# A new order of all engines, two products in four column tiles, and the expert turns written out

## Chip, core and metric

The kernel runs on one core of a Trainium2 chip (trn2). The metric is the device time of one execution in microseconds, median of three runs of the kernel before: 1279.1 us (1278.93 to 1279.16). Less is better.

## What is computed

128 samples; each has 64 image patches, one class token and 32 text tokens of width 128, so 97 tokens.

```python
h = concat(tokens(x), txt)                     # patches @ W, + b, * positions; 97 tokens of 128
h = h + retention(layernorm(h))                # complex, 8 heads of 16, decay mask, group norm, gate
h = h + ffn(layernorm(h))
def ffn(x):
    o = softmax(q k^T / 4) v @ Wo + bo         # 8 heads of 16
    t = layernorm(x + o)
    e, gw = argmax, max of softmax(t @ gate_W + gate_b)
    return gw * (gelu(t @ W1[e] + b1[e]) @ W2[e] + b2[e])      # one of 8 experts per token
```

All of it is float32.

## The kernel before

Four samples make a group (388 tokens); there are NG = 32 groups. The first stage is a software pipeline over groups, written out by hand for each engine: one iteration `i` of `for i in range(FIRST, STEADY)` is a list of steps, each for the group `i - lag` (`at(step, i - lag)`). After the loop each engine has a list of its own for the last groups. Nothing but the order in these lists and the semaphores sets the order of the work. The steps with A are the first attention, B the second, C the third normalization and the routing.

- TensorE: `ahead(g, c0, c1)` is part of the embedding of a coming group (19 chunks of 128x128 weights by 256 columns, L479). `a_scores`, `b_scores`, `b_shifted` (L550, L614, L637) use four row tiles of 32 rows of the array. `a_mix`, `b_mix`, `b_sums` (L564, L667, L649) use four column tiles of 32 columns. All else uses the whole array, among it `product` (L460) with 128x128 weights by 388 columns: `a_q_real`, `a_q_imag`, `a_gate`, `a_out`, `b_q`, `b_k`, `b_wo`. `b_hrows` is L681, `c_rows` L690, `b_max_t` L624, the bfloat16 `c_rank` L698 and L701. A float32 product is two matmul instructions in the trace, a float32r one is one.
- PSUM has eight banks: emb, x, y, z and s0 to s3. `USES` and `LAST_USES` name the bank of each step. A step waits until the holder before it has been drained.
- VectorE: `a_decayed` and `b_max` over 776 columns, the routing (`place_all` to `place_index`, which gives the row in HBM of each token), and more.
- ScalarE: logs, exponentials, and the copies out of PSUM into `row_sb`: `b_row_copy` (L1120) and `c_row_copy` (L1127). `row_sb` has ROWS = 3 buffers, so both wait in `free_rows(g)` until the scatter of group g - 3 has landed.
- GpSimd: `text(g)` copies text tokens; `scatter(g)` (L1909) writes the rows of group g to HBM (`expert_rows`), four indirect DMAs of 97 rows. It waits for `place_index(g)`, the gate weight, the token numbers and `b_row_copy(g)`.

In the second stage 104 tiles of 128 tokens, 13 turns of 8 slots, go through the expert network: TensorE turns a tile (L825), makes the hidden layer (L832) and the output (L843); VectorE copies weights (L1844, L1846) and makes the result (L1853 to L1859); GpSimd writes it to the output with an indirect DMA (L1926). In `result(n, s)` of a turn n > 0 VectorE waits until the output of the same slot in the turn before has landed. TensorE's turns 0, 1 and 12, and VectorE's too, are written out; the others are loops of the hardware (`Fori`), ScalarE's from turn 1 on. The expert phase begins when `place_index(NG - 1)` and `run_on(NG - 1)` are done.

The lines that set the two waits which matter below:

```python
def free_rows(g):
    if g >= ROWS:
        act.wait_ge(s_scat[g % ROWS], 16 * G * (g // ROWS))
...
def result(n, s):
    ...
    if later(n):
        dve.wait_ge(s_out[s], 16 * n)
```

Of the kernel before, what the change touches and what calls it, by code (L numbers as in the profile page):

```python
# [55 lines left out]
def _pack(*fields):  # L56
# [35 lines left out]
    ("A.scores2.0", "s0 s1", NG - 1), ("A.scores2.1", "s2 s3", NG - 1), ("B.q", "y", NG - 2), ("B.o", "z", NG - 3),  # L92
    ("A.scores3.0", "s0 s1", NG - 1), ("A.scores3.1", "s2 s3", NG - 1), ("B.den", "y", NG - 3),
    ("B.scores1.0", "s0 s1", NG - 2), ("B.scores1.1", "s2 s3", NG - 2), ("B.scores0.0", "s0 s1", NG - 2),
    ("B.scores0.1", "s2 s3", NG - 2), ("A.yvar", "y", NG - 1), ("B.wo", "z", NG - 3), ("B.v", "s0", NG - 2),
    ("B.max_t0", "y", NG - 2), ("B.hrows", "x", NG - 2), ("A.out", "s2", NG - 1), ("C.rank", "z", NG - 4),
    ("B.max_t1", "s3", NG - 2), ("C.rows0", "s0", NG - 3), ("C.rows1", "s1", NG - 3), ("B.center", "y", NG - 1),
    ("B.shifted1.0", "s0 s1", NG - 2), ("B.shifted1.1", "s2 s3", NG - 2), ("B.var", "z", NG - 1),
    ("B.shifted0.0", "s0 s1", NG - 2), ("B.shifted0.1", "s2 s3", NG - 2), ("B.k", "z", NG - 1), ("B.q", "s2", NG - 1),
    ("B.den", "s1", NG - 2), ("C.rank", "s0", NG - 3), ("B.o", "y", NG - 2), ("B.scores1.0", "s0 s1", NG - 1),  # L100
    ("B.scores1.1", "s2 s3", NG - 1), ("B.wo", "y", NG - 2), ("B.max_t1", "z", NG - 1),
    ("B.scores0.0", "s0 s1", NG - 1), ("B.scores0.1", "s2 s3", NG - 1), ("C.rows1", "y", NG - 2),
    ("C.rows0", "x", NG - 2), ("B.max_t0", "z", NG - 1), ("B.shifted1.0", "s0 s1", NG - 1),
    ("B.shifted1.1", "s2 s3", NG - 1), ("B.shifted0.0", "s0 s1", NG - 1), ("B.shifted0.1", "s2 s3", NG - 1),
    ("B.v", "x", NG - 1), ("B.den", "s1", NG - 1), ("B.o", "x", NG - 1), ("C.rank", "s2", NG - 2),
    ("B.wo", "z", NG - 1), ("C.rows0", "s0", NG - 1), ("C.rows1", "s3", NG - 1), ("B.hrows", "z", NG - 1),
    ("C.rank", "s0", NG - 1),
]
STEADY = NG
# [24 lines left out]
def counts(order):  # L134

    seen, n = {}, 0
    for i in range(FIRST, LAST):
        for *what, lag in order:
            if 0 <= i - lag < NG:
                n += 1  # L140
                seen[(i - lag, *what)] = n
    return seen
# [3 lines left out]
    ("exp_sum", 4), ("place_all", 4), ("place_chosen", 4), ("place_sum", 4), ("place_index", 4), ("logit_max", 3),  # L146
    ("top", 3), ("top_index", 3), ("first_top", 3)]
ROUTE = counts(ROUTE_ORDER)
# [13 lines left out]
def fusion(nc, x_main, x_tail, w_main, w_tail, txt_t, pos_t, consts, weights, columns, token_no,  # L162
           exp_w1, exp_w2, no_token, out, rows, table):
    with ExitStack() as ctx:
# [286 lines left out]
        def _(pe):  # L451
# [75 lines left out]
            def a_q_real(g):  # L527
                read(pe, g, "A.center")
                product(g, "A.qr", ar[:], xn[:, g % 2, :])

            def a_q_imag(g):
                read(pe, g, "A.center")
                product(g, "A.qi", ai[:], xn[:, g % 2, :])

            def a_gate(g):
                read(pe, g, "A.center")
                product(g, "A.gate", weight("w1"), xn[:, g % 2, :])
# [37 lines left out]
            def a_out(g):  # L575
                pe.wait_ge(s_yn, g + 1)
                product(g, "A.out", weight("w2"), yn[:])
# [7 lines left out]
            def b_q(g):  # L585
                read(pe, g, "B.center")
                product(g, "B.q", weight("Wq"), x2[:, g % 2, :])

            def b_k(g):
                read(pe, g, "B.center")  # L590
                product(g, "B.k", weight("Wk"), x2[:, g % 2, :])

            def b_values(g):
                read(pe, g, "B.center")
                ps = use(g, "B.v")
                for c in range(4):
                    mm = pe.matmul(ps[0:S, c * P:(c + 1) * P], x2[:, g % 2, c * S:(c + 1) * S], weight("Wv"),  # L597
# [277 lines left out]
        def _(act):  # L875
# [368 lines left out]
            for s in range(SLOTS):  # L1244
                hidden(0, s)
# [791 lines left out]
```

## Time and profile before

| | |
|---|---|
| median of 3 runs | 1279.1 us |
| the profiled execution | 1277.0 us, its span 1275.0 us |
| TensorE busy | 97% (matmuls), weight loads 73% |
| VectorE, ScalarE, GpSimd busy | 78%, 62%, 32% |
| DMA | 98 GB/s in the mean, 16 engines a third busy |
| mean granted TensorE clock | 0.991 |

The span is the time from the first instruction to the last in the profiled execution; 2 us lie around it. Busy shares are of the span. The granted clock is a share of full speed: 1.00 is 2.4 GHz, 0.50 is 1.2 GHz. The chain of work is followed back from the last instruction, at each step to what released it.

### The profile page before, as it was taken

The numbers are of one execution on the slowest core, as the hardware profiler recorded it, in microseconds if no ns is written. First come the engines' busy times: TensorE is split into PE (matmuls) and PEld (weight loads), VectorE is DVE, ScalarE is ACT, GpSimd is POOL, SyncE is SP. The second block draws the span as 40 slices with busy tenths as digits, with TensorE's granted clock in tenths as the row PEclk, the third lists the DMA queues.
The fourth block names the chain that finished last, engine by engine and source line by source line (L and its number), as shares of the span: only waits on it lengthen the run. The fifth ranks groups of instructions, "written<-read, shape, count | busy, mean of one in ns | idle before, by whom it ended". The sixth has DMA issues, their size and how long they took to land.

```text
span 1275.0 us, 43269 instructions
## 1 busy us (share of the span) xinstructions
PE 1240.5 (97%) x15924; PEld 930.4 (73%) x15925; DVE 998.1 (78%) x2447; ACT 794.3 (62%) x1787; POOL 410.5 (32%) x268
## 2 busy tenths in 40 slices
PE   8999999999999999999999999999999876999998
PEld 6667777777777777777777777777776556999998
DVE  3678888888888888888888888888888766777776
ACT  2466666666666666666666666666666664556555
POOL 0000322232222222222222222222222146666666
PEclk9999999999999999999999999999999898999999
DMA  9522333333333333333333333333330013443332
GB/s 387 188 83 80 93 93 93 93 93 93 93 93 93 93 93 93 93 93 93 94 92 93 93 93 94 93 93 94 93 93 16 14 17 89 135 114 102 103 103 62
DMA packets 95146, 124.80 MB, mean 98 GB/s; under 512 B 56619, under 2 KB 77149, under 8 KB 94592
## 3 DMA queue, kind: packets, MB, share of 16 engines
q1 hardware_dynamic: 38400, 102.47, 25.4%
q0 software_dynamic: 56576, 19.93, 7.5%
q8 instruction: 122, 2.00, 0.7%
q14 instruction: 48, 0.39, 0.1%
HBM read 101.27 MB, written 20.82 MB: 96 GB/s over the span
## 4 chain that ended last, share of the span: by engine, by line
PE 80%; DVE 6%; issue 5%; DVEq 3%; POOL 2%; DMA 2%; ACT 1%; SPq 0%; POOLq 0%; ACTq 0%
PE bank_emb L479 22%; PE bank_s L550 10%; PE bank_x L564 7%; PE bank_y L460 7%; PE bank_s L637 4%; PE bank_s L614 4%; PE bank_z L460 4%; PE bank_y L649 3%; PE bank_y L667 3%; DVEq L1842 2%; PE bank_z L597 2%; DVE home_x L1846 2%; PE bank_s L460 2%; PE bank_y L690 1%; PE bank_s L843 1%
## 5 line engine op out<-in xcount | busy, mean ns | idle before, releaser
L1909 POOL DMA_INDIRECT expert_rows<-row_sb,placei x128 | 278.1, 2173 | 562.8 <-issue 464.8
L479 PE MATMUL bank_emb<-home_x 128*128 128x256 f32 x1216 | 338.1, 392 | 0.0
L479 PEld LDWEIGHTS bank_emb<-home_x 128*128 128x128 f32 x1216 | 210.3, 189 | 81.9 <-issue 56.5
L1374 DVE TENSOR_TENSOR home_s<-bank_s,con 97x776 f32<-97x776 f32 x256 | 239.3, 956 | 22.9 <-PE bank_s L550 22.8
L1926 POOL DMA_INDIRECT out_tokens<-yo,tok x104 | 122.9, 1181 | 69.7 <-issue 52.7
L1391 DVE TENSOR_REDUCE mx<-bank_s 97x8 f32<-97x776 f32 x128 | 117.7, 961 | 30.8 <-PE bank_s L614 30.6
L1102 ACT ACTIVATE home_s<-bank_s 97x776 f32<-97x776 f32 x128 | 97.5, 814 | 59.5 <-PE bank_s L637 59.5
L550 PE MATMUL bank_s<-qm,xn 32*97 32x452 f32 x1024 | 131.4, 580 | 1.7 <-DVE vp L1381 1.2
L564 PEld LDWEIGHTS bank_x<-home_s,vp 97*32 97x32 f32 x4096 | 90.0, 110 | 33.2 <-issue 29.4
L564 PE MATMUL bank_x<-home_s,vp 97*32 97x97 f32 x4096 | 111.8, 249 | 1.2 <-DVE vp L1381 1.2
L843 PE MATMUL bank_s<-w2e,home_s 128*128 x832 | 109.8, 275 | 0.0
L843 PEld LDWEIGHTS bank_s<-w2e,home_s 128*128 128x128 f32 x832 | 101.3, 192 | 0.0
L1241 ACT ACTIVATE home_s<-bank_x,home_x 128x128 f32<-128x128 f32 x208 | 59.3, 367 | 46.6 <-PE bank_x L832 37.5
L1241 ACT ACTIVATE home_s<-bank_y,home_x 128x128 f32<-128x128 f32 x208 | 59.3, 368 | 43.8 <-PE bank_y L832 39.3
L1381 DVE COPY vp<-bank_s 97x128 f32<-97x128 f32 x256 | 67.5, 284 | 23.5 <-PE bank_s L550 23.1
L1896 POOL COPY h<-txt 128x128 f32<-128x128 f32 x32 | 9.4, 292 | 230.2 <-DVE h L1429 206.6
L550 PEld LDWEIGHTS bank_s<-qm,xn 32*97 32x97 f32 x1024 | 34.2, 158 | 45.0 <-issue 36.5
L637 PE MATMUL bank_s<-qx,kx 32*97 32x97 f32 x2048 | 60.9, 255 | 3.5 <-ACT home_s L1102 1.7
L637 PEld LDWEIGHTS bank_s<-qx,kx 32*97 32x97 f32 x2048 | 50.4, 162 | 19.0 <-issue 14.6
L614 PE MATMUL bank_s<-k,q 32*97 32x194 f32 x1024 | 60.3, 341 | 1.2 <-DVE mx L1391 0.7
L1066 ACT ACTIVATE kx<-bank_z,kx_bias,con 128x194 f32<-128x194 f32 x128 | 59.5, 528 | 2.5 <-PE bank_z L460 2.5
L832 PE MATMUL bank_x<-home_s,home_x 128*128 128x128 f32 x416 | 56.5, 280 | 3.2 <-DVE home_x L1846 3.0
(297 smaller groups left out, 2369.9 us busy)
## 6 DMA issues: line engine op xcount, KB each, us to landing
home_x<-in_x_main SPq DMA_DIRECT2D x96, 768.0 KB, 4.5
home_x<-expert_rows SPq DMA_DIRECT2D x104, 129.0 KB
w1e<-in_exp_w SPq DMA_DIRECT2D x1, 2576.0 KB, 13.2
txt<-in_txt_t SPq DMA_DIRECT2D x32, 64.0 KB, 3.6
w2e<-in_exp_w SPq DMA_DIRECT2D x1, 2048.0 KB, 17.6
expert_rows<-row_sb,placei POOLq DMA_INDIRECT x128, 8.7
out_tokens<-yo,tok POOLq DMA_INDIRECT x104
home_x<-in_x_tail SPq DMA_DIRECT2D x32, 48.0 KB, 3.4
```

Of the source, the lines that this page charges most:

```text
L460: done(pe.matmul(ps[:, 0:N], lhs, rhs, start=True, stop=True), g, name)
L479: mm = pe.matmul(banks["emb"][:, 0:NPG], wtok[:, c, :], x_sb[:, c, :], start=(c == 0), stop=(c == KC - 1))
L550: mm = pe.matmul(bank_s[0:S, r, 0:4 * S + 64], xn[rows32, g % 2, t], qm[rows32, k, :], start=True, stop=True)
L564: mm = pe.matmul(ps[32 * r:32 * r + 32, k * S:(k + 1) * S], v, sm[:, k % 2, r, j * S:(j + 1) * S], start=(j == 0), stop=(j == 3), skip_gro ...
L614: mm = pe.matmul(dst, q2[rows32, t], k2[rows32, :, t], start=True, stop=True)
L637: mm = pe.matmul(bank_s[0:S, r, j * S:(j + 1) * S], kx[rows32, o, t], qx[rows32, o, t], start=True, stop=True)
L843: mm = pe.matmul(banks[bank_o[s % 2]][:, 0:P], hid[:, s, f, :], w[:, f * P:(f + 1) * P], start=(f == 0), stop=(f == FB - 1))
L1241: act.activation(hid[:, s, f, :], banks[bank_h[s % 2]][:, f * P:(f + 1) * P], ACT.Gelu_apprx_tanh, bias=w1b[:, s, FF + f:FF + f + 1]).then ...
L1374: ins = dve.tensor_tensor(sm[:, k % 2, 2 * h:2 * h + 2, :], pair(h), decay, ALU.mult)
L1391: drain(dve.tensor_reduce(mx[:, k, :].rearrange("p (r j z) -> p r j z", j=4, z=8)[:, 2 * h:2 * h + 2, :, 0], pair(h).rearrange("p g (j t) ...
L1909: pool.indirect_dma_start(out=rows[:, :], out_offset=bass.IndirectOffsetOnAxis(ap=placei[:, k, c:c + 1], axis=0), in_=row_sb[:, k, c, E:E ...
L1926: pool.indirect_dma_start(out=out, out_offset=bass.IndirectOffsetOnAxis(ap=tok[:, s, :], axis=0), in_=yo[:, s, :], in_offset=None, bounds_ ...
```

## The change

1. All lists of steps, for TensorE, ScalarE, VectorE and GpSimd, have another order, and so have `USES`, `LAST_USES` and the numbering of routing steps. The loop ends an iteration sooner (`STEADY = NG - 1`), the lists for the end are longer by it. ScalarE and VectorE start their iteration at another point of the cycle.
2. `b_q` and `b_k` are made in four column tiles (`split=True`), beside `b_sums`, `b_mix` and `a_mix`.
3. `place_index(g)` comes later on VectorE, behind `b_normal` and `c_scale`; `place_all` and `place_chosen` come sooner. Two waits are added (`logits` for the exponentials of the group before, `place_sum` for the `place_index` of the group before).
4. GpSimd's scatters at the end come in another order.
5. The expert turns of TensorE, VectorE and ScalarE are written out instead of looped.

```diff
-            def product(g, name, lhs, rhs):
+            def product(g, name, lhs, rhs, split):
                 ps = use(g, name)
-                done(pe.matmul(ps[:, 0:N], lhs, rhs, start=True, stop=True), g, name)
+                for c in range(0, P, 32) if split else ():
+                    mm = pe.matmul(ps[c:c + 32, 0:N], lhs[:, c:c + 32], rhs, start=True, stop=True)
+                if not split:
+                    mm = pe.matmul(ps[:, 0:N], lhs, rhs, start=True, stop=True)
+                done(mm, g, name)
```

TensorE's loop afterwards (the loop before is printed above):

```python
a_scores(i-1, 2); ahead(0, 1); b_sums(i-3, 0), (1); a_mix(i-1, 1); a_scores(i-1, 3)
b_q(i-2, split=True); b_mix(i-3, 0); a_mix(i-1, 2); b_mix(i-3, 1); a_mix(i-1, 3)
b_scores(i-2, 1); a_center(i); ahead(1, 3); b_wo(i-3); ahead(3, 5); a_var(i); c_rank(i-4); ahead(5, 7)
b_scores(i-2, 0); a_yvar(i-1); ahead(7, 8); a_q_real(i); c_rows(i-3, 0); ahead(8, 9); b_max_t(i-2, 1)
b_hrows(i-2); c_rows(i-3, 1); a_q_imag(i); b_shifted(i-2, 1); a_out(i-1); ahead(9, 10); b_values(i-2)
a_scores(i, 1); ahead(10, 12); b_center(i-1); b_max_t(i-2, 0); ahead(12, 13); a_gate(i)
a_scores(i, 0); ahead(13, 15); b_var(i-1); ahead(15, 18); b_shifted(i-2, 0); ahead(18, 19)
a_mix(i, 0); b_k(i-1, split=True)
```

```diff
-    ("B.scores1.1", "s2 s3", 2), ("B.wo", "y", 3), ("A.var", "s2", 0),
-    ("B.max_t1", "s0", 2), ("B.hrows", "y", 2), ("C.rows1", "x", 3), ("B.shifted1.0", "s0 s1", 2),
+    ("C.rows0", "z", 3), ("B.max_t1", "s1", 2), ("B.hrows", "s0", 2), ("C.rows1", "z", 3), ("A.qi", "x", 0),
+    ("B.shifted1.0", "s0 s1", 2), ("B.shifted1.1", "s2 s3", 2), ("A.out", "z", 1), ("B.v", "y", 2),
...
 # ScalarE, loop
-                at(a_query, i, 1)
-                at(a_query, i, 0, last=True)
-                at(b_row_copy, i - 2)
-                at(c_row_copy, i - 3, 1)
-                at(b_exp, i - 2, 1, 0)
+                at(y_rstd, i)
+                at(a_query, i + 1, 0)
+                at(c_row_copy, i - 2, 0)
+                at(a_query, i + 1, 1, last=True)
+                at(b_row_copy, i - 1)
+                at(c_row_copy, i - 2, 1)
+                at(c_square, i - 2)
...
 # VectorE, loop
-                at(place_all, i - 4)
-                at(run_on, i - 4)
-                at(place_chosen, i - 4)
-                at(place_sum, i - 4)
-                at(h0_low_ahead, i)
-                at(gate_weight, i - 4)
-                at(place_index, i - 4)
-                at(a_decayed, i - 1, 3, 0)
...
                 at(b_normal, i - 1)
-                at(gate_times, i)
-                at(tokens_ahead, i + 1)
                 at(c_scale, i - 3)
+                at(place_index, i - 4)
                 at(logits, i - 3)
...
 # GpSimd
             for i in range(FIRST, STEADY):
+                at(text, i + 1)
                 at(scatter, i - 4)
-                at(text, i + 1)
-
+
+            scatter(NG - 5)
             scatter(NG - 4)
+            scatter(NG - 1)
+            scatter(NG - 2)
             scatter(NG - 3)
-            scatter(NG - 2)
-            scatter(NG - 1)
...
 # TensorE, expert turns (VectorE and ScalarE alike)
-            with pe.Fori(2, TURNS1) as n:
+            for n in range(2, TURNS1):
                 turn(n)
             pe.wait_ge(s_list, 2)
-            with pe.Fori(TURNS1, TURNS - 1) as n:
-                turn(n)
-            turn(TURNS - 1, True)
+            for n in range(TURNS1, TURNS):
+                turn(n, n == TURNS - 1)
```

## Rows read from the trace of the kernel before

**Rows 1.** The page, section 1: busy time, share of the span, instructions.
```profile
PE 1240.5 (97%) x15924; PEld 930.4 (73%) x15925; DVE 998.1 (78%) x2447; ACT 794.3 (62%) x1787; POOL 410.5 (32%) x268
```

**Rows 2.** Chain of work, one steady iteration: start us, us, what.
```profile
433.35 1.06 PE bank_emb L479 x4
...
434.59 0.18 PE bank_z L468
434.76 1.73 PE bank_emb L479 x8
...
440.40 1.46 PE bank_y L649 x32
...
456.61 0.46 PE bank_x L690 x4
457.07 0.87 PE bank_s L637 x32
...
465.02 1.06 PE bank_emb L479 x4
```

**Rows 3.** Timeline of a steady iteration, VectorE, ScalarE, GpSimd: start us, us, engine.
```profile
444.20 0.14 DVE L1546 CAST placei<-placef 97x4 int32<-97x4 f32 x1
...
467.64 0.56 DVE L1334 TENSOR_TENSOR x<-bank_x,rsb 128x388 f32<-128x388 f32 x1 [0.28 <-ACT rsb L923]
...
456.70 0.59 ACT L1120 COPY row_sb<-bank_y 97x512 f32<-97x512 f32 x1
...
445.58 2.17 POOL L1909 DMA_INDIRECT expert_rows<-row_sb,placei  x1 [17.30 <-issue]
...
452.97 2.15 POOL L1909 DMA_INDIRECT expert_rows<-row_sb,placei  x1 [0.30 <-issue]
```

**Rows 4.** L1909: landing after the start, all; then two windows, a group's fourth.
```profile
DMA to landing us min/median/max: 6.9/8.7/12.5
...
DMA to landing us min/median/max: 12.5/12.5/12.5
...
DMA to landing us min/median/max: 10.2/10.2/10.2
```

**Rows 5.** Timeline around the first expert turns: last placement, scatters, first outputs.
```profile
1061.73 0.17 DVE L1546 CAST placei<-placef 97x4 int32<-97x4 f32 x1
...
1061.46 2.15 POOL L1909 DMA_INDIRECT expert_rows<-row_sb,placei  x1 [6.37 <-DVE place L1519]
...
1081.14 1.00 POOL L1926 DMA_INDIRECT out_tokens<-yo,tok  x1 [0.30 <-issue]
...
1090.02 0.15 DVE L1857 COPY tok<-home_x 128x1 int32<-128x1 int32 x1 [2.23 <-DMA out_tokens<-yo,tok]
...
1091.54 1.16 PE L832 MATMUL bank_x<-home_s,home_x 128*128 128x128 f32 x8 [1.27 <-DVE home_x L1846]
```

**Rows 6.** Windows: stretch, its length, busy time of PE, PEld, DVE, ACT, POOL, clock, DMA.
```profile
950.00:1061.50 111.50, 94.29 (x1451) 63.10 (x1450) 83.74 (x221) 69.20 (x141) 35.22 (x18) 0.95 0.12 22
...
1005.00:1010.00 5.00, 5.00 (x59) 2.27 (x62) 1.52 (x8) 4.37 (x8) 0.00 (x0) 0.54 0.00 0
...
1101.30:1118.00 16.70, 16.30 (x139) 15.59 (x137) 11.63 (x41) 9.28 (x33) 9.48 (x8) 1.00 0.47 129
...
1133.10:1148.40 15.30, 15.30 (x139) 15.30 (x137) 11.19 (x40) 9.13 (x33) 9.68 (x9) 1.00 0.36 103
```

**Rows 7.** TensorE's timeline: the fill, the last iteration of the loop, two expert tiles.
```profile
41.57 1.02 PE L550 MATMUL bank_s<-qm,xn 32*97 32x452 f32 x8 [0.94 <-DVE vp L1381]
...
977.71 1.02 PE L550 MATMUL bank_s<-qm,xn 32*97 32x452 f32 x8
...
1007.87 1.84 PE L550 MATMUL bank_s<-qm,xn 32*97 32x452 f32 x8
...
1095.44 1.06 PE L832 MATMUL bank_x<-home_s,home_x 128*128 128x128 f32 x8
...
1097.33 1.06 PE L832 MATMUL bank_y<-home_s,home_x 128*128 128x128 f32 x8
```

More of the change, by code:

```diff
@@ L131, with counts @@
     take(_g, _use)
-def counts(order):
+def counts(order, last):
     seen, n = {}, 0
-    for i in range(FIRST, LAST):
+    for i in range(FIRST, STEADY):
         for *what, lag in order:
@@ L573, in a_yvar, with a_out @@
                 halves(g, "A.yvar", "sqy", mean_head_r[:], y_hi[:], y_lo[:])
-            def a_out(g):
+            def a_out(g, split=False):
                 pe.wait_ge(s_yn, g + 1)
-                product(g, "A.out", weight("w2"), yn[:])
+                product(g, "A.out", weight("w2"), yn[:], split)
             def b_center(g):
@@ L596, in b_values @@
                 for c in range(4):
-                    mm = pe.matmul(ps[0:S, c * P:(c + 1) * P], x2[:, g % 2, c * S:(c + 1) * S], weight("Wv"),
-                                   start=True, stop=True)
+                    for a in range(0, S, 32 if split else S):
+                        b = min(a + 32, S) if split else S
+                        mm = pe.matmul(ps[a:b, c * P:(c + 1) * P], x2[:, g % 2, c * S + a:c * S + b], weight("Wv"),
+                                       start=True, stop=True)
                 done(mm, g, "B.v")
@@ L682, in b_hrows, with c_rows @@
                 done(mm, g, "B.hrows")
-            def c_rows(g, half):
+            def c_rows(g, half, split=False):
                 read(pe, g, "B.wo")
@@ L722, in _ @@
                 at(a_mix, i - 1, 1)
-                at(c_rank, i - 4)
-                at(ahead, i + 1, 0, 1)
-                at(b_q, i - 2)
                 at(a_scores, i - 1, 3)
-                at(ahead, i + 1, 1, 2)
-                at(a_center_ahead, i)
+                at(b_q, i - 2, split=True)
+                at(b_mix, i - 3, 0)
                 at(a_mix, i - 1, 2)
-                at(b_mix, i - 3, 0)
                 at(b_mix, i - 3, 1)
@@ new lines, in _ @@
+            a_mix(NG - 2, 1)
+            b_sums(NG - 4, 0)
+            b_sums(NG - 4, 1)
+            a_scores(NG - 2, 3)
+            b_q(NG - 3, split=True)
+            b_mix(NG - 4, 0)
+            a_mix(NG - 2, 2)
+            b_mix(NG - 4, 1)
+            a_mix(NG - 2, 3)
+            b_scores(NG - 3, 1, first=True)
+            a_center(NG - 1)
+            b_wo(NG - 4)
+            a_var(NG - 1)
+            c_rank(NG - 5)
+            a_yvar(NG - 2)
+            b_max_t(NG - 3, 1)
+            c_rows(NG - 4, 0)
@@ new lines, in _ @@
+            a_q_real(NG - 1)
+            b_scores(NG - 3, 0)
+            b_hrows(NG - 3)
+            c_rows(NG - 4, 1)
+            a_out(NG - 2)
+            a_q_imag(NG - 1)
+            b_shifted(NG - 3, 1)
+            b_max_t(NG - 3, 0)
+            b_values(NG - 3)
+            a_scores(NG - 1, 1, first=True)
+            b_center(NG - 2)
+            a_gate(NG - 1)
+            a_scores(NG - 1, 0)
+            b_var(NG - 2)
+            b_shifted(NG - 3, 0)
+            a_mix(NG - 1, 0)
@@ L768, in _ @@
+            b_k(NG - 2, split=True)
+            a_scores(NG - 1, 2)
             a_mix(NG - 1, 1)
-            b_q(NG - 2)
-            b_mix(NG - 3, 0)
+            b_q(NG - 2, split=True)
             a_scores(NG - 1, 3)
             a_mix(NG - 1, 2)
+            c_rank(NG - 4)
             b_sums(NG - 3, 0)
@@ L1242, in hidden @@
                                    bias=w1b[:, s, FF + f:FF + f + 1]).then_inc(s_gelu, 1)
[L1244 to L1246 removed]
+            for n in range(TURNS):
                 for s in range(SLOTS):
@@ new lines, in _ @@
+            b_query_max(NG - 3, 1, 0)
+            b_query_max(NG - 3, 1, 1, last=True)
+            y_normal(NG - 2)
+            place_sum(NG - 5)
+            y_gated(NG - 2)
+            place_index(NG - 5)
+            b_max(NG - 3, 0, 1)
+            b_max(NG - 3, 0, 0)
+            a_residual(NG - 2)
+            a_query_imag(NG - 1, 0)
+            a_query_imag(NG - 1, 1, last=True)
+            c_sum(NG - 4)
+            h1_low(NG - 2)
+            b_query_max(NG - 3, 0, 1)
+            a_value_rows(NG - 1, 1, 1)
@@ new lines, in _ @@
+            a_decayed(NG - 1, 1, 0)
+            a_value_rows(NG - 1, 1, 0, last=True)
+            a_decayed(NG - 1, 1, 1, last=True)
+            b_query_max(NG - 3, 0, 0, last=True)
+            b_low(NG - 2)
+            gate_one(NG - 1)
+            a_value_rows(NG - 1, 0, 1)
+            a_decayed(NG - 1, 0, 1, last=True)
+            a_value_rows(NG - 1, 0, 0)
+            a_decayed(NG - 1, 0, 0, last=True)
+            b_normal(NG - 2)
+            c_scale(NG - 4)
+            logits(NG - 4)
@@ L1734, in _ @@
             one_hot(NG - 4)
             a_decayed(NG - 1, 3, 1)
-            a_value_rows(NG - 1, 3, 1, last=True)
             a_decayed(NG - 1, 3, 0)
             a_value_rows(NG - 1, 3, 0, last=True)
+            a_value_rows(NG - 1, 3, 1, last=True)
+            place_all(NG - 4)
+            gate_weight(NG - 4)
+            place_chosen(NG - 4)
+            run_on(NG - 4)
+            place_sum(NG - 4)
+            token_numbers(NG - 4)
+            place_index(NG - 4)
+            next(first, None)
```

428 lines of the change are left out of this document (242 added, 186 removed), and 13 rows, old and new, of the table USES.

## Prediction

> **What bounds the kernel.** Read the busy times first: TensorE is busy 97% of the span, VectorE 78%, ScalarE 62%, GpSimd 32% [rows 1]. Then the chain of work over one iteration of the pipeline: it runs through TensorE alone, and an iteration takes 465.02 - 433.35 = 31.67 us [rows 2]. So in the steady stretch, about 30 iterations, only TensorE's own time counts, as long as no other engine makes it wait. Then the timeline of the other engines, for the chains that run beside it [rows 3, 4], and last the expert phase, where tiles follow at 1097.33 - 1095.44 = 1.89 us [rows 7] and where the first turns show a wait on GpSimd [rows 5].
>
> **Part 1: mode switches and the split products.** Eight embedding instructions of 256 columns with no change of tiles ahead of them take 1.73 us, so four need 0.86 and a column 0.84 ns; four behind a row-tiled step take 1.06 [rows 2]. `b_sums`, 32 instructions of 194 columns in four tiles side by side, needs 32 / 4 x 194 x 0.84 ns = 1.31 and takes 1.46 behind row tiles [rows 2]. So each change between whole array, row tiles and column tiles costs about 0.2 us. The old cycle has 19 such changes, the new one 18: `c_rank` no longer stands between column tiles and the whole array, and the split `b_q` joins `b_mix`, but `ahead(0, 1)` now cuts between `a_scores` and `b_sums`. I take -0.14 us an iteration, between 0 and -0.3.
>
> The split itself I cost at nothing: 8 instructions of 388 columns, 0.33 us each by the same rate, need 8 / 4 x 0.33 = 0.65 us in four tiles, what two whole ones need. `b_sums` would need 32 x 0.16 = 5.2 us without overlap and takes 1.46 [rows 2]; so column tiles do run side by side, even with both halves of a product issued one after the other. If they did not here, each product would cost 1 us more, 2 with no overlap at all (a rival).
>
> **Part 2: the wait that the order of VectorE adds.** Here is the step that decides. `row_sb` has three buffers. `b_row_copy(g)` must wait until the scatter of g - 3 has landed, and what waits for the copy is new: `B.hrows` now lies in bank s0, which `b_shifted(g, 1)` takes next, so TensorE itself waits. Behind the waiting copy on ScalarE are queued `c_row_copy`, `c_square` and the exponentials; behind `b_shifted` all of TensorE. Before, `place_index` ran at 444.20 and the fourth DMA of its scatter, started at 452.97, landed near 464; the copy that needed it came at 456.70 + 31.67 = 488.4 [rows 2, 3], 24 us later. Now it stands behind `b_normal` and `c_scale`, a whole iteration later in effect.
>
> The chain, from the end of `b_var` on TensorE (434.59 + 0.18 = 434.77, one iteration on 466.44 [rows 2]): `b_normal` starts 1.20 later at 467.64 [rows 3]; `b_normal` 0.48 and `c_scale` 0.65, an estimate from their rows of that length; `place_index` 0.14; then 444.34 to 445.58 = 1.24 until GpSimd's first DMA starts [rows 3]; 452.97 - 445.58 = 7.39 to the start of the fourth [rows 3]; its landing, 10.2 to 12.5 after its start, 11.35 in the mean of the ten that are recorded, whose ends are shown [rows 4]; the copy, 0.59 [rows 3]; 0.15 for two semaphores. Sum 23.2, from 22.0 to 24.3.
>
> TensorE's own way between the same two steps: before, 457.07 - 434.77 = 22.30 [rows 2]. The same 13 embedding chunks lie in it; one `c_rows` comes in (+0.46 [rows 2]), the saving of part 1 goes out. 22.6. So it waits 0.6 us, and up to 1.7 where a landing is late. The wait returns every time, since `place_index` moves with it. The iteration becomes 31.67 - 0.14 + 0.6 = 32.13, +0.46. It needs g of 3 and more: 26 iterations, +12.0; four others -0.14 each. **Steady: +11.5.** An error of 0.5 us in either sum moves this from about 3 to 24.
>
> Against this stands a rule: the Trainium skill, "DMA: Bandwidth & Descriptors", section "Anatomy of one DMA — SWDGE (gpsimd) path", fits a GpSimd DMA as 2.0 us plus its bytes over 436 KB per us. By that the fourth would land some 2.2 us after its start, the chain would take 14, and nothing would wait. The recorded landings, 8.7 in the median over all [rows 4], do not bear it out for these scattered rows. It belongs to the first rival.
>
> **Part 3: fill and drain.** In the fill TensorE already waits for VectorE between scores and sums, 0.94 us in one place [rows 7]. The new order has one embedding chunk there where the old had more, and less of the second attention to cover it in its first two iterations: +2, from 0 to +4. The iteration without embedding (1007.87 - 977.71 = 30.2 us [rows 7]) loses nine chunks, 3.8 us, from TensorE's way in part 2 but nothing from the chain: it would wait 4.3, of which the old one already loses a part to VectorE: +3, from 0 to +5. The last lists hold the same work with the same last chain; 0, from -4 to +4. The two added waits in the routing hit steps whose releaser ran long before: nothing.
>
> **Part 4: GpSimd's order at the end.** Before, the scatters of groups 30 and 31 start at 1061.46 and the first output DMA at 1081.14, so eight DMAs take 19.68, 2.46 each [rows 5]. It lands 8.9 us on; VectorE waits 2.23 us for it in the first result of turn 1, and TensorE idles 1.27 [rows 5]. Now `scatter(NG - 1)` stands first. It needs the very last `place_index`, whose counterpart is at 1061.73 [rows 5], so 12 DMAs start at 1063.14 and end at 1092.66. **+11.5** for the first output, and VectorE's wait and TensorE's next tile move by the same 11.5. TensorE then idles some 14 us. After gaps of the drain the granted clock was 0.54, near the level of 1.2 GHz, over 5 us [rows 6]; 3 to 7 us at half speed cost 1.5 to 3.5: +2.5.
>
> **Part 5: turns written out.** Turn 2, the first of the loop, took 16.7 us, a later one 15.3 [rows 6]; eight tiles at 1.89 are 15.16. Gain 1.4 + 10 x 0.2 = -3.4. The new code must be fetched; turns 0 and 1 are written out already and show 1.89 [rows 7], so nothing; at worst 0.45 a turn as at a loop's entry, +5. Expert phase: 11.5 + 2.5 - 3.4 = **+10.6**.
>
> **Sum.** 11.5 + 2 + 3 + 0 + 10.6 = +27.1. The profiled execution took 1277.0 and becomes 1304.1; the median lies 2.1 above it: **1306** (1279.1 + 27.1 = 1306.2).
>
> **Rivals.**
> (a) The scatter lands in time; only part 4 costs. For it: the two sums of part 2 are 0.6 apart, each good to 0.5. Then -0.14 x 30 = -4.2, +2, +1, +10.6: +9.4, 1288.5. Chance 0.2.
> (b) Faster: the drain is packed. From 950 to 1061.5 TensorE idles 111.5 - 94.3 = 17.2 us [rows 6]. If the longer lists for the end fill all of it, the last placement comes 17 us sooner, and that outweighs part 4; with no wait of part 2, it decides from 10.6 + 2.6 = 13.2 us on. 17 us give -17 + 10.6 = -6.4: 1272.7. Against it: the last idle stretch is the routing of the last group, one chain in both orders, and VectorE is busy 84 us of that stretch itself. Chance 0.1.
> (c) The split overlaps only in part: each second half waits for its first, five steps of 0.32, so a product takes 1.6 instead of 0.65. The wait of part 2 hides 0.6 of the two; (2 x 0.97 - 0.6) x 30 = +40 on top: 1346. Against it: `b_sums` [rows 2]. The Trainium skill, "TensorEngine Tiling (Array Packing)", section "Restrictions and Gotchas", says that column tiling disables fast weight load; no row here shows that it costs anything. Chance 0.05.
> (d) The pieces cancel, within 0.2% of 1279.1: half of that idle time is filled and (a) holds. Chance 0.05.
>
> **Chances and range.** My forecast 0.60, its own range 1292 to 1324, from the bounds of part 2 (-8.5 to +12.5), of the drain and of the clock. With (a) the range reaches down to 1284 and up to 1324. 0.2% (2.6 us) is about what a measurement of this kernel can tell from no change: faster by more 0.10 from (b), within 0.05 from (d), slower by more 0.85 from the rest.
>
> **What the new profile would show.** Part 1: the cycle without waits at 31.5. Part 2: a wait of TensorE before L637's counterpart each iteration, released by ScalarE's `b_row_copy`, itself released by the scatter; an iteration of 32.1. Part 4: twelve scatters in a row, first output 31 us after the last placement, one idle stretch of about 14 us on TensorE. Part 5: tiles 1.89 apart with no step at turns. Wrong would be: 31.5 with no wait (part 2 is then mis-sized), or more than 33 (landings later than recorded).

## The result and the profile after

| | before | after |
|---|---|---|
| median of the runs, us | 1279.01 (1276.95 to 1279.16) | 1313.76 (1308.95 to 1319.96) |
| profiled execution, us | 1277.0 | 1308.95 |
| its span, us | 1275.0 | 1307.1 |

The changed kernel is slower: ratio 1.028, 95% interval 1.023 to 1.033. The forecast was 1306 with a range from 1284 to 1324. Its runs lie 11 us apart, those of the kernel before, beside them, 2. The profiled execution is the fastest of the four, so what follows explains 32 us of the 34.8 between the medians; what the others lost beyond it is in no profile.

The page of the changed kernel, section 1 (busy time, share, instructions) and parts of section 4 (shares of the chain that ended last). It answers to [rows 1].

```profile
PE 1245.3 (95%) x16308; PEld 926.6 (71%) x16308; DVE 1007.4 (77%) x2446; ACT 791.8 (61%) x1787; POOL 409.8 (31%) x268
...
PE 68%; DMA 11%; POOL 7%; issue 5%; DVE 5%; ACT 3%; SPq 0%; DVEq 0%; POOLq 0%; ACTq 0%
```

TensorE still works 1245 us, but it is no longer the whole chain: scatters on GpSimd and their landings are 18% of it.

**Where the 32 us are.** I cut both spans at marks that every iteration has. The first is VectorE's write of the normalised images (`xn`). Here are its 27 instructions from the 5th to the 31st group as one line of the trace: durations, then first and last start. The kernel before:

```profile
L1329 DVE TENSOR_TENSOR xn<-bank_z,rsa x27: 561/561/561, 136.2 to 959.5; 128x388 f32<-128x388 f32 x27
```

The changed kernel:

```profile
L1412 DVE TENSOR_TENSOR xn<-bank_y,rsa x27: 548/551/554, 139.6 to 978.2; 128x388 f32<-128x388 f32 x27
```

Experiment e1 below, four row buffers:

```profile
L1412 DVE TENSOR_TENSOR xn<-bank_y,rsa x27: 550/552/554, 138.1 to 964.7; 128x388 f32<-128x388 f32 x27
```

Those 26 intervals take 823.3 us before, 838.6 after, and 826.6 in e1: +15.3 for the change. The start up to the 5th group costs +3.4. The rest is the end: the last group's `xn` stands at 990.1 before and at 1009.2 after, so what follows it takes 284.9 and 297.9: +13.0. With 0.4 in the interval in between that is the 32. All these marks are read from one profile of each kernel.

### The profile page after: what moved, and what is told of

It reads as the page before. It is cut to its first block, busy times and chain, and to the rows that moved or that the text cites. A ratio compares the mean times of both kernels' runs of the same rounds, so it can differ in the third digit from the quotient of the medians.

```text
span 1307.1 us, 43299 instructions
## 1 busy us (share of the span) xinstructions
PE 1245.3 (95%) x16308; PEld 926.6 (71%) x16308; DVE 1007.4 (77%) x2446; ACT 791.8 (61%) x1787; POOL 409.8 (31%) x268
## 4 chain that ended last, share of the span: by engine, by line
PE 68%; DMA 11%; POOL 7%; issue 5%; DVE 5%; ACT 3%; SPq 0%; DVEq 0%; POOLq 0%; ACTq 0%
PE bank_emb L510 16%; DMA expert_rows<-row_sb,placei 10%; PE bank_s L581 8%; POOL expert_rows L2032 6%; PE bank_s L913 6%; PE bank_x L595 4%; PE bank_s L670 4%; PE bank_x L902 3%; PE bank_z L490 3%; PE bank_y L902 3%; PE bank_s L647 3%; PE bank_y L490 3%; PE bank_y L630 2%; PE bank_y L682 2%; PE bank_z L700 2%
## 5 line engine op out<-in xcount | busy, mean ns | idle before, releaser
L510 PEld LDWEIGHTS bank_emb<-home_x 128*128 128x128 f32 x1216 | 214.1, 190 | 97.4 <-issue 64.0
L1464 DVE COPY vp<-bank_s 97x128 f32<-97x128 f32 x256 | 64.6, 283 | 20.5 <-PE bank_s L581 17.5
L670 PEld LDWEIGHTS bank_s<-qx,kx 32*97 32x97 f32 x2048 | 50.0, 161 | 38.1 <-ACT row_sb L1189 22.6
L1155 ACT ACTIVATE qx<-bank_y,qx_col 128x388 f32<-128x388 f32 x62 | 41.9, 676 | 50.1 <-PE bank_y L488 50.1
L670 PE MATMUL bank_s<-qx,kx 32*97 32x97 f32 x2048 | 60.6, 254 | 10.1 <-ACT row_sb L1189 5.7
```

The source lines that it names most:

```text
L510: mm = pe.matmul(banks["emb"][:, 0:NPG], wtok[:, c, :], x_sb[:, c, :], start=(c == 0), stop=(c == KC - 1))
L670: mm = pe.matmul(bank_s[0:S, r, j * S:(j + 1) * S], kx[rows32, o, t], qx[rows32, o, t], start=True, stop=True)
```

## What the steady iterations lose

Single starts in the timeline show what the mean hides. Before, all 26 intervals are 31.67. After, nine are 31.60 or 31.61, three lie from 31.25 to 31.67, and fourteen between 31.8 and 36.2. So the iteration itself became a little shorter (31.62, the value of nearly all in e1), and single ones are long. They are long for two reasons. An interval is named below after the group that it begins with: the 9th runs from the 9th group's `xn` to the 10th's.

**The row copy.** Who waited for whom, changed kernel, over the whole span (us in total, times, longest):

```profile
PEld bank_s L670 <- ACT row_sb L1189: 22.6, 29, 2.1
...
ACT row_sb L1189 <- DMA expert_rows<-row_sb,placei: 14.2, 17, 2.0
...
PE bank_s L670 <- ACT row_sb L1189: 5.7, 9, 1.5
```

That is the wait that the prediction put into part 2: TensorE's `b_shifted` behind ScalarE's `b_row_copy` behind the scatter of three groups before. The first row counts weight loads, the third products. The kernel before has none of the three. With four buffers (e1) the second and the third are gone and the first is 16.0 in 29, 0.6 at the longest: what is left is the normal distance to the copy. So the wait costs TensorE 22.6 - 16.0 = 6.6 us here; the products alone show 5.7, in nine waits. The chain of the changed kernel through one such iteration:

```profile
581.88 12.40 DMA expert_rows<-row_sb,placei
...
594.30 0.59 ACT row_sb L1189
...
607.68 2.17 POOL expert_rows L2032
...
615.06 11.74 DMA expert_rows<-row_sb,placei
```

From the copy to the next scatter 13.38, to the fourth DMA 7.38, its landing 11.74: 32.5, where a free iteration takes 31.62. The loop closes as forecast, but only a landing of more than 31.62 - 13.38 - 7.38 = 10.86 us makes TensorE wait. The trace of the changed kernel has no landing of a fourth DMA beside the ones on its chain. In e1, where the scatters stand at the same place, eight are recorded: 9.8 to 12.5 us, 10.8 in the mean, four of them below 10.86. The nine of the kernel before in its steady part had 11.4 in the mean, two of them below.

**Stops with no releaser.** The intervals exceed 31.62 by 838.6 - 26 x 31.62 = 16.5 us in all. 6.6 are the row copy. The other 9.9 are stops of TensorE 26 to 29 us behind the `xn` that opens the iteration, for which the trace shows no releaser, and the lower clock behind two of them (a granted clock of 0.5 for 3.4 us each, after the stops of 1.5 us in the 9th and the 28th interval). The timeline of TensorE in the interval that took 35.1 us:

```profile
292.78 0.52 PE L700 MATMUL bank_z<-home_s,vp 97*32 97x97 f32 x16
293.12 0.84 PE L595 MATMUL bank_x<-home_s,vp 97*32 97x97 f32 x30
295.45 0.35 PE L595 MATMUL bank_x<-home_s,vp 97*32 97x97 f32 x2 [1.49 <-issue]
```

It stops between the 30th and the 31st of 32 equal instructions; no semaphore stands there. The DMA view of the 0.2 us from 293.1: packets that start in it, MB, their share of the time of 16 engines:

```profile
q8 instruction: 1, 0.02, 29.9%
```

One packet of the instruction queue, 16384 bytes; 29.9% of 16 x 0.2 us is 0.96 us, and from its start at 293.16 it ends at 294.12. TensorE goes on 1.33 us behind that. By the packet records this holds for all 29 stops of this kind with over 0.4 us of idle time in the 26 intervals of the ten kernels with the new order (changed, e1, e2, e7 to e12, e14): TensorE resumes 1.21 to 1.48 us behind the end of an instruction packet. The kernel before has packets too, 104 from 80 to 1000 us, and no such stop; nor have e5 and e13, which keep its order. What differs is how dense the work is: the most instructions that TensorE starts within 6 us of one iteration (weight loads, products and a few others) are 324 before and 401 after, and the stops lie in the last part of that stretch or right behind it (`b_sums`, `a_mix`, split `b_q`, `b_mix`). What differs too is where the scatters lie; e2 and e11 below bear on both.

The Trainium skill, "Runtime: NRT & Kernel Launch", section "Instruction fetch mechanics", says that an engine's instructions are refilled in blocks of 16 KiB, 256 instructions, and that crossing a block border is mostly hidden. The packet size here agrees; that it is hidden holds for the order before and not for this one.

## What the end loses

VectorE's last placements in the changed kernel (timeline: start, us). With the two fences that follow they answer to [rows 5].

```profile
1076.42 0.16 DVE L1633 CAST placei<-placef 97x4 int32<-97x4 f32 x1
...
1079.39 0.17 DVE L1633 CAST placei<-placef 97x4 int32<-97x4 f32 x1
...
1080.42 0.17 DVE L1633 CAST placei<-placef 97x4 int32<-97x4 f32 x1
```

GpSimd's scatters and the first output DMA, the same timeline:

```profile
1043.84 2.15 POOL L2032 DMA_INDIRECT expert_rows<-row_sb,placei  x1 [0.30 <-issue]
1081.84 2.14 POOL L2032 DMA_INDIRECT expert_rows<-row_sb,placei  x1 [35.85 <-issue]
...
1094.13 2.15 POOL L2032 DMA_INDIRECT expert_rows<-row_sb,placei  x1 [0.30 <-issue]
1099.32 2.15 POOL L2032 DMA_INDIRECT expert_rows<-row_sb,placei  x1 [3.04 <-issue]
...
1111.59 2.15 POOL L2032 DMA_INDIRECT expert_rows<-row_sb,placei  x1 [0.31 <-issue]
1114.05 1.00 POOL L2050 DMA_INDIRECT out_tokens<-yo,tok  x1 [0.30 <-issue]
```

GpSimd idles 35.85 us and then has twelve scatters in a row. The first output leaves 33.5 us behind the last placement, before 19.2: +14.2. The forecast was +11.5; the 2.7 more are the gap of 3.04 in the queue. It stands ahead of the seventh scatter of the twelve, the third of its group, where GpSimd's program waits for nothing. e2 and e8 have it too, of 5.14 and 4.01 us, and e1, with twelve in a row as well, has none. Its cause is open. One thing was not forecast: groups 29, 30 and 31 are placed within 4 us. In the kernel before, group 29's placement ends at 1044.3, 17.6 us ahead of the last. So the queue does not hang on GpSimd's order alone; VectorE places group 29 late.

TensorE's expert tiles behind it, first product of a tile each:

```profile
1111.63 1.16 PE L902 MATMUL bank_y<-home_s,home_x 128*128 128x128 f32 x8 [0.29 <-DVE home_x L1970]
1124.43 2.08 PE L902 MATMUL bank_x<-home_s,home_x 128*128 128x128 f32 x8 [10.63 <-DVE home_x L1970]
1128.22 1.77 PE L902 MATMUL bank_y<-home_s,home_x 128*128 128x128 f32 x8
1130.83 1.06 PE L902 MATMUL bank_x<-home_s,home_x 128*128 128x128 f32 x8
1132.72 1.06 PE L902 MATMUL bank_y<-home_s,home_x 128*128 128x128 f32 x8
```

TensorE is idle for 10.63 us (forecast 14), then two tiles come of 3.79 and 2.61 instead of 1.89 at a granted clock of 0.5, the level of 1.2 GHz: 2.6 us lost, the forecast said 2.5. The thirteenth tile stands 115.2 us behind the last `xn`, before 101.5. The 91 tiles from it to the last take 175.2 (1299.63 - 1124.43) against 176.05: -3.4 by the turns, +2.5 by the clock.

## The experiments

**Four row buffers (e1).** The scratch tile of the lists moves so that the fourth fits.
```diff
-ROWS = 3
+ROWS = 4
-        spread = sb("spread", [P, 2, NT])
+        spread = view(gate, 0, 2, NT)
```


> The changed kernel with four buffers for the rows instead of three (the scratch tile of the tile lists moves into a dead tile to make room); nothing else. Theory (the copy of a group's rows waits until the scatter of three groups before has landed, and TensorE waits for that copy): the wait before the row copy is gone, every steady interval is 31.6 us, so the profiled 1308.95 loses the 15 us by which its 27 intervals exceed 31.6: about 1294 us, and the runs of this kernel agree within 1 us where those of the changed kernel lie 11 us apart. The end (twelve scatters queued) stays. Rival (the longer iterations come from the new order or the clock, and the wait only shows it): within 3 us of the changed kernel, runs still apart.

Measured: 1297.57 (1293.59 to 1301.98), 1.016 times before, interval 1.012 to 1.020; 16 us below the changed kernel, expected were 20 (1294). The profiled 26 intervals take 826.6. The wait is gone as expected, and the theory of part 2 stands. Of the gain in the profile, 15.3 us, 12.1 lie in these intervals; 1.9 lie behind the last `xn`, where the gap in the queue of scatters is missing. But five intervals are still long (4.4 us), and the runs are still 8 us apart: the copy was not the only reason, and not the one for the spread. On this chip the kernel before also spread, from 1274.7 to 1281.5, so I draw nothing further from spreads.

**The placement early (e2), and late (e8).** In e2 `place_index` stands behind `place_sum`; in e8 it is moved the other way, behind `top`.
```diff
                 at(place_sum, i - 4)
+                at(place_index, i - 4)
...
-                at(place_index, i - 4)
```


> The changed kernel with the one conversion place_index moved from behind c_scale to right behind place_sum in VectorE's loop, 13.6 us earlier (464.3 instead of 477.8); GpSimd then starts the scatter behind its text copy, about 8.7 us earlier. Three row buffers stay. Theory: the scatter lands more than the 0.6 us plus jitter earlier that is needed, the wait goes, and the time is that of four buffers, about 1294 us, with runs within 1 us. If a whole landing more than 8 us longer than the usual one is behind the long intervals, some stay. Rival (order or clock): within 3 us of the changed kernel.

Measured: 1304.45 (1301.95 to 1308.47), 10 above the expected 1294. The wait of the copy for the scatter is gone, the row `PEld bank_s L670` is 16.0 as with four buffers, and the 26 intervals take 828.8. That is the gain of e1 in the steady part. The total is 7 us above e1. In the profiles 5.2 us more lie in the end, where VectorE waits 15.6 us for the first output, and 2.4 in the start. The 5.2 in the end are the gap ahead of the seventh scatter, here 5.14 us where e1 has 0.30 (GpSimd's timeline of e2):

```profile
1094.20 2.34 POOL L2032 DMA_INDIRECT expert_rows<-row_sb,placei  x1 [5.14 <-issue]
```

Of the 2.4 in the start 1.3 lie ahead of the first `xn` and 1.1 behind it, where the granted clock of e2 is 0.5 from 46.4 to 49.8 us and that of e1 is not. The edit should touch none of this, and why it comes is open.

e2 also says something on the stops. TensorE's program is that of e1 and of the changed kernel, so the packets' borders are the same; only the scatters lie elsewhere, 8.7 to 18.2 us behind an iteration's `xn` instead of 17.6 to 27. The stops of over 0.4 us lie in the 14th, 18th, 19th, 20th, 23rd and 24th interval. In e1 they lie in the 9th, 22nd and 28th, in the changed kernel in the 6th, 9th, 12th and 28th. Each is one profile, but e9, with the loop of e1, has all five of its long intervals again (the 6th, 9th, 12th, 22nd and 28th). One of e2 (TensorE's timeline), 1.42 us behind the end of a packet:

```profile
451.26 0.62 PE L700 MATMUL bank_z<-home_s,vp 97*32 97x97 f32 x19 [1.11 <-issue]
```

So the borders alone don't seem to decide which packet comes late; where the scatters lie counts too.

The other edit:
```diff
-                at(place_index, i - 4)
...
                 at(top, i - 3)
+                at(place_index, i - 4)
```


> The changed kernel with place_index moved 3.4 us later still in VectorE's loop, behind the step top (the start of the scatter moves from 479.2 to about 482.6 in the iteration shown). Theory (a closed chain: placement, scatter, landing, row copy, TensorE, scaling, placement, as long as the iteration): every steady iteration grows by about 3.3 us, from 31.6 to 34.9, so some 85 us in all less the 15 that it already has: 1385 us (1370 to 1400). Rival (the wait is a by-product with slack in it): under 10 us.

Measured: 1439.89, 126 us above the changed kernel, where the edit added some 2.4 us to the placement (533.9 against 531.5 for the end of `c_scale`). Most intervals are 37 to 38 us. Its chain of work through one of them:

```profile
505.14 12.72 DMA expert_rows<-row_sb,placei
517.88 0.60 ACT row_sb L1189
518.52 1.25 PE bank_s L670 x32
...
535.31 2.17 POOL expert_rows L2032
...
542.70 12.70 DMA expert_rows<-row_sb,placei
```

17.43 from the copy to the scatter, 7.39, 12.70: 37.5, the whole interval. Against the changed kernel's 13.38 + 7.38 + 11.74 the first part is 4.05 longer: 2.4 by the edit and the rest because TensorE, idle some 4 us in each iteration, runs what follows at the lower level of its clock (32 products of L670 in 1.25 instead of 0.94). The direction was right, the size (1385) too small by 55 us, outside the 1370 to 1400 expected: a closed chain charges every microsecond each time, and the clock charges again.

**The end in another order (e7), and with four buffers (e9).**
```diff
             b_rstd(NG - 1)
+            c_log(NG - 3)
+            c_rstd(NG - 3)
...
             b_normal(NG - 1)
+            c_scale(NG - 3)
+            logits(NG - 3)
...
-            scatter(NG - 1)
-            scatter(NG - 2)
             scatter(NG - 3)
+            scatter(NG - 2)
+            scatter(NG - 1)
```


> The changed kernel with another end: group 29's routing (c_scale to place_index, its logarithm, exponentials and rank product) comes as soon as its square sums are there, some 15 us earlier, and GpSimd scatters the last groups in the order 29, 30, 31. Steady iterations are unchanged. Theory (twelve scatters at 2.46 us queue behind the last placement where eight did): four of the twelve move ahead of the last placement, so the first output DMA comes about 20 us behind it instead of 33.5, and the time falls by 10 to 14 us against the changed kernel, to about 1297 beside a changed kernel at 1309. Rival (the queue is hidden, what follows it was bound by the tiles anyway, since TensorE's thirteenth tile is only late because tiles follow at 2.45 us beside the scatters): no more than 4 us.

Measured: 1304.22 (1301.28 to 1309.21), 9.5 below the changed kernel, just under the 10 to 14 expected. From the last `xn` to the end 286.6 us against 297.9, although the last placement itself came 5 us later (76.4 behind the last `xn`, 71.4 before the edit: group 29's placing now stands in the way of `c_rows`). The first output leaves 19.8 us behind it. So the end gained 11.3 us in the profile, 2.6 of them because TensorE's clock no longer falls behind its idle stretch; the steady part of this run was 3.6 us longer.

> The changed kernel with both edits together: four row buffers, and the end in which group 29 is routed early and the scatters go 29, 30, 31. Everything else, the split products and the written-out turns too, is the changed kernel's. Theory (the loss is the row-copy wait plus the queue of scatters at the end, and the two are independent): the stretch from the 5th to the 31st group takes about 827 us as with four buffers alone (838.6 in the changed kernel), the stretch from the last group's normalisation to the end 285 to 289 us (297.9), so about 1284 us in total, 0.3 to 0.8% above the kernel before. Rival (one hides behind the other): about 1290 or more.

Measured: 1287.82 (1286.67 to 1288.38), 1.007 times before, interval 1.005 to 1.009; expected were 1284. The two edits add up: 16.2 and 9.5 alone, 25.9 together. End 283.1, steady 831.6 with seven long intervals; one of them, 37.1 us, began with a stop of TensorE of this kind and went on at the lower clock. The steady part is 4.6 us longer than expected, by these stops alone: its copy never waits for a scatter.

**The split products (e10) and the stops (e11, e12, e14).**
```diff
-                at(b_q, i - 2, split=True)
+                at(b_q, i - 2)
...
-                at(b_k, i - 1, split=True)
+                at(b_k, i - 1)
```


> The kernel of e9 with every product for queries and keys whole again, no four column tiles; the order is unchanged. Theory of the mode changes (each change between whole array, row tiles and column tiles costs TensorE about 0.2 us): two changes more in each iteration, so 31.6 becomes about 32.0 and the time grows by 8 to 11 us. Rival (the split products' 14 further instructions in each iteration cause the stops of 0.4 to 2.4 us without any releaser that TensorE shows right behind its densest stretch, 4.4 us over the steady part with four buffers): those stops go, and the time grows by less, 4 to 7 us.

Measured: 1297.18 (1296.01 to 1299.01), 9.4 above e9, within the 8 to 11 of the theory. Every undisturbed iteration takes 32.01 instead of 31.62: +0.39 for two more changes of tiling, 0.20 each, the price of part 1. The stops took 9.4 us in e9 and take 5.5 here, 4.4 of it in one interval; e1 with the split had 4.4 in all, so that is no difference. The split saves 10 us, and the stops do not come from it.

The edit of e11 upon e10:
```diff
                 at(b_q, i - 2)
+                at(ahead, i + 1, 1, 5)
...
-                at(ahead, i + 1, 1, 3)
                 at(b_wo, i - 3)
-                at(ahead, i + 1, 3, 5)
```


> The kernel of e10 with four embedding chunks of the next group (1 to 4) moved from behind a_center_ahead and b_wo to right behind the whole b_q, into the stretch in which TensorE issues 466 instructions within 8 us. Mode changes are those of e10. Rival (TensorE outruns its instructions in that stretch): the stops without releaser are gone where e10 still has them, 2 to 5 us below e10. If they have nothing to do with the dense stretch: within 1 us of e10.

Measured: 1335.87, 39 above e10; expected were 2 to 5 below, or no change. One stop remains (1.3 us), but the iteration is 33.37. Who waited for whom in e11, 150 to 1000 us:

```profile
PE bank_s L526 <- ACT a_hi L983: 13.2, 25, 0.5
PE bank_s L528 <- DVE a_lo L1409: 7.4, 25, 0.3
```

The moved chunks had covered the squaring between `a_center` and `a_var`; without them TensorE waits there each time, 0.5 and 0.3 us of the 1.36 by which the iteration grew; the rest is not traced. That the chunks hid this was overlooked. Whether fewer stops came because of density stays unproven by this run: its densest 6 us hold 316 instructions, fewer than the 324 of the kernel before, which has no stop, and one came all the same. So a density under that of the kernel before is not enough to be rid of them.

The edit of e12 upon e9:
```diff
+            for _ in range(64):
+                pe.matmul(warm[:, 0:8], zeros[:, 0:P], zeros[:, 0:8], start=True, stop=True)
```


> The kernel of e9 with 64 tiny products of zeros (8 columns each, results never read) behind the ten warming products at the start, where TensorE waits for the first images anyway; all later work is the same, only its place in TensorE's instruction stream moves by 128 instructions. Theory (the stops of 0.2 to 3 us right behind the densest stretch come when the next packet of the instruction queue arrives late, and so hang on where the packet borders fall): the long iterations, the 6th, 9th, 12th, 22nd and 28th interval in the changed kernel, in the one with four buffers and in e9, move to other numbers or go, their sum changes by some us either way, and TensorE again resumes 1.2 to 1.4 us behind the end of an instruction packet. Rival (the stops belong to those groups' data or loads): the same numbers stay long. Total within 8 us of e9.

Measured: 1313.24, 25 above e9, where at most 8 were expected. The first `xn` stands at 49.2 instead of 25.8; from there on the two profiles take 1260.8 and 1260.4. That the start would hide them was wrong; TensorE's timeline of e12:

```profile
7.91 22.92 PE L560 MATMUL bank_x<-home_s 128*128 128x8 f32 x128
```

128 products and as many weight loads: 256 instructions, one whole packet. The intervals 6, 9, 12 and 28 were long again, the 8th and the 15th were new, and the 18th, 22nd and 25th of e9 were free. That looked like the rival, but the dose was badly chosen: it leaves the borders where they were.

> The kernel of e12 with 32 tiny products instead of 64. The 64 had become 128 weight loads and 128 products in the trace, 256 instructions, so all borders between instruction packets of 16384 bytes fell where they had fallen before: the packets started at the same places of each iteration as with four buffers, and the 6th, 9th, 12th and 28th interval were long again. 32 shift the borders by half a packet. Theory (a stop comes where a packet border falls into the dense stretch so that the packet of 24 us into the iteration is asked for late): with 3.69 packets in an iteration the borders of the intervals 6, 9, 12, 22, 25 and 28 come to lie in others, and the long intervals are among the 7th, 11th, 14th, 17th, 20th, 24th, 27th and 30th, while the 6th, 9th, 12th and 28th are 31.6. TensorE again resumes 1.2 to 1.5 us behind the end of a packet. Total about 1300, the 11.5 us of the tiny products above e9. Rival (the stops belong to the groups themselves): the 6th, 9th, 12th and 28th interval stay long.

Measured: 1300.69, as expected. Long are now the 11th, 14th, 17th, 20th, 23rd and 26th, every third, and the 27th and 28th; the 6th, 9th and 12th are 31.62. Five of the eight numbers named came true; the 23rd was expected as the 24th, and the 28th stayed. The data and the groups are the same; the borders of the packets moved. With that the stops are shown to hang on where the borders fall, though not on that alone (e2), and by one profile of this kernel, taken on another chip than that of e9. That the 28th stayed long is not explained. TensorE's timeline at one of them:

```profile
843.11 0.68 PE L626 MATMUL bank_x<-home_s,vp 97*32 97x97 f32 x23
845.30 0.44 PE L626 MATMUL bank_x<-home_s,vp 97*32 97x97 f32 x9 [1.51 <-issue]
```

And the DMA view of e14, the 0.3 us from 842.8 (20.2% of 16 x 0.3 us is 0.97 us; from 842.91 it ends at 843.88, and TensorE resumes 1.42 us on):

```profile
q8 instruction: 1, 0.02, 20.2%
```

What stays open is why the packet comes late: the density of the stretch, the scatter's small packets beside it (in the changed kernel GpSimd scatters from 17.6 to 27 us into the iteration and the densest 10 us begin at 16.6; before, they overlap by 3 us), or both. e2 shows that moving the scatters moves the stops, with density and borders unchanged; e11 shows that a less dense stretch still has one. No run takes the scatters away from the dense stretch altogether.

**The turns alone (e5), and a try to beat both (e13).**
```diff
-            with pe.Fori(2, TURNS1) as n:
+            for n in range(2, TURNS1):
                 turn(n)
```


> The kernel before with only the expert turns written out on TensorE, ScalarE and VectorE. Theory: the steps at the loop borders between tiles go, 3.4 us less (the prediction's part 5). Rival: the loop borders are hidden, within 1 us of the kernel before. This run's span also tells what the same steady part and the same end as before take on this chip.

Measured: 1275.09 (1271.57 to 1278.42), 0.9968 times before, interval 0.9950 to 0.9986. From the thirteenth tile to the last 172.7 us against 176.0: -3.4, as the prediction had it. It is the only version whose whole interval lies below 1, by 0.3%.

The edit of e13 upon e5:
```diff
             place_all(NG - 2)
+            gate_weight(NG - 2)
...
             one_hot(NG - 1)
-            gate_weight(NG - 2)
```


> The kernel before with the expert turns written out and one instruction moved: gate_weight of group 30 (the reciprocal that releases that group's scatter at 1065.8, 7.4 us behind its placement at 1058.4) from behind the routing of group 31 to right behind place_all of group 30. Theory (the queue of scatters at the end sets when the first outputs leave, as the changed kernel showed from the other side): group 30's four DMAs start about 6 us earlier, the eight end about 5 us earlier, and the time is 3 to 5 us less than with the turns alone: about 1271 us, faster than both kernels. Rival (the tiles would not have gone faster anyway): within 1 us of the kernel with the turns alone, 1275.

Measured: 1276.03 (1273.08 to 1278.98), 0.9988 times before, interval 0.9973 to 1.0004. The scatters moved as planned (group 30's starts at 1059.6 instead of 1065.8, the last one 6.5 us earlier), and in the profile the part behind the last `xn` is 2.9 us shorter. The medians do not show it, with runs that lie 6 us apart. The expectation of 3 to 5 us did not come true; whether nothing or some 2 us was gained stays open.

## Why the prediction was right, and where it was not

The forecast of 1306 against 1313.8, with the range around it and the sign, held. The terms of the end (parts 4 and 5) were right for their reasons; the steady part came out near its size with only about half of its reason, and that is luck.

- **Part 1.** 0.2 us for a change of tiling is right (e10: 0.39 / 2). The iteration lost 0.05 us, not 0.14, although the trace has the 19 and 18 changes that were counted; what takes the rest back is not shown. The split costs nothing; without it the change would have cost 10 us more. Rival (c), by which a split product takes 1.6 us, is out. The chain of the changed kernel shows the two of an iteration:

```profile
447.50 0.65 PE bank_z L488 x8
...
452.80 0.79 PE bank_y L488 x8
```

- **Part 2.** The mechanism is there, with its place and its releasers, and two ways of taking it away (e1, e2) give 826.6 and 828.8 for the steady part. The size failed: I took the mean landing, 11.35, as each one's, and so a wait of 0.6 in every iteration. With the 10.8 of e1 the loop takes 13.38 + 7.38 + 10.8 = 31.6 and waits only for a landing longer than the mean. The trace shows no wait beyond the usual 0.6 in many of them and up to 2.1 in others, in all 6.6 us over 26, not the 15.6 of 26 x 0.6. That the steady part still came out at +15.3 against +11.5 is owed to the stops, 9.9 us, which no step of the prediction had. So the sum was nearly right by luck, with a term of 9 us too large and one of 9.9 missing.
- **The rule against it**, by which the fourth DMA would land 2.2 us behind its start: the landings on the chain are 11.7 and 12.4 us in the changed kernel. Rival (a), with its steady part free of the wait, is what e1 shows, and there too the time was 1297.6, not 1288.5, with 4.4 us of stops, the start (+3 beyond the first `xn`) and the twelve scatters in it.
- **Part 3.** Start +3.4 (forecast +2). The last lists: -0.4 from the last `xn` to the last placement, and 0.4 for the iteration ahead of it; +3 was forecast. The chain of the row copy did not bite there. Rivals (b) and (d) wanted 17 us and half of that out of the drain; the 0.4 that came rule both out.
- **Part 4.** First output +14.2 for +11.5; half-speed loss 2.6 for 2.5. TensorE's thirteenth tile moved by 13.7 behind the last `xn`. Right, except that VectorE's late placing of group 29 makes the queue as much as GpSimd's order does. The order alone was not run.
- **Part 5.** -3.4, exact.

## What to carry to other kernels

Where a buffer comes free by a slow DMA, and what refills it leads back to that DMA, compare the length of the closed chain with the iteration, with the late landings and not the mean one: below the iteration it costs nothing, above it every microsecond counts each time. Count what queues behind the last result on the engine that also starts the outputs, and ask which engine placed that work so late. And where TensorE is idle without a releaser behind a stretch of many short instructions, lay the instruction packets beside it before explaining it by the data.

## What the runs showed of the hardware

- TensorE's instructions arrive in packets of 16384 bytes, 3.6 in an iteration of 918 instructions before and 3.7 in one of 942 after (882 and 906 of them weight loads and products). In the steady iterations of the new order it stopped at some of them for 0.4 to 2.6 us, and resumed 1.21 to 1.48 us behind the packet's end. Which ones moved when the borders moved (e14) and when the scatters did (e2).
- 8 columns are not cheap: a product of 8 columns in fp32 with its own 128x128 weights took 0.36 us at the start (22.9 us for 64, two passes each), mostly at the granted clock of 0.5.
- VectorE's copy of the expert weights takes longer while GpSimd scatters. The group of that copy in the changed kernel (count, busy us and mean ns, idle before), during the scatters from 1082 to 1114 us:

```profile
L1970 DVE COPY home_x<-w1e 128x644 f32 x12 | 12.0, 1000 | 0.0
```

Behind them:

```profile
L1970 DVE COPY home_x<-w1e 128x644 f32 x87 | 42.2, 485 | 0.1
```

1000 ns against 485, and tiles then follow at 2.45 us, the scatters' distance, instead of 1.89. The Trainium skill, "SBUF — State Buffer", section "SBUF: two separate sides", says that such an fp32 copy and GpSimd's descriptor writing exclude each other for a whole instruction. The doubled copies fit that. So does e2: in the 5.14 us in which GpSimd idles between two scatters, three of these copies take 0.48 to 0.49 us. No run takes the scatters away altogether.
